# Four graph-attention layers on one core: the second half of each adjacency tile converted by POOL instead of DVE during the first pass

## What is computed

```python
h = jnp.einsum('nf,hfd->hnd', x, W)
e = jax.nn.leaky_relu(s_src[:, :, None] + s_dst[:, None, :], 0.01)
e = jnp.where(adj[None, :, :] == 0, -jnp.inf, e)
alpha = jax.nn.softmax(e, axis=-1)
out = jnp.einsum('hij,hjd->hid', alpha, h)
return jax.nn.elu(out)
```

## Time and profile before

| | |
|---|---|
| median of 3 runs | 3547.81 us (3545.58 to 3547.96) |
| the profiled execution's own time | 3546.96 us |
| its span | 3545.0 us |
| DVE busy over the span | 2442.6 us (69%) |
| PE busy over the span | 3075.2 us (87%) |
| POOL busy over the span | 1355.8 us (38%) |

### The profile page before, as it was taken

One profiled execution on the slowest core, in us unless ns is written; L12 is line 12 of the kernel. 1 busy time (PEld: TensorE's weight loads), 2 busy tenths in 40 slices (PEclk: granted clock), 3 DMA queues, 4 the chain that ended last, 5 costly groups with the idle time before them and its releaser, 6 DMA issues.

```text
span 3545.0 us, 75493 instructions
## 1 busy us (share of the span) xinstructions
PE 3075.2 (87%) x26666; PEld 2775.1 (78%) x26666; DVE 2442.6 (69%) x4181; ACT 1671.2 (47%) x2980; POOL 1355.8 (38%) x1770
## 2 busy tenths in 40 slices
PE   6688899999649999999969999968888888559998
PEld 5688899999639999999958888845565555449998
DVE  4888788887778888887765444347777777564446
ACT  4456788998548899889830000012222222230000
POOL 2433455532234555552210000025555555524443
PEclk9799999999879999999989999979999999779999
DMA  7564000000000000000010000010000000000001
GB/s 260 182 241 156 10 12 13 12 13 17 1 7 12 12 13 12 13 12 11 13 60 10 18 12 15 16 34 6 6 6 6 6 6 6 3 0 1 0 0 47
DMA packets 48448, 113.41 MB, mean 32 GB/s; under 512 B 8176, under 2 KB 29168, under 8 KB 40176
## 3 DMA queue, kind: packets, MB, share of 16 engines
q1 hardware_dynamic: 48368, 112.35, 9.5%
HBM read 103.75 MB, written 8.59 MB: 32 GB/s over the span
## 4 chain that ended last, share of the span: by engine, by line
PE 60%; DVE 23%; issue 8%; POOL 3%; DMA 2%; ACT 2%; DVEq 1%; SPq 1%; POOLq 0%; ACTq 0%
PE bank L933 15%; PE bank L936 15%; PE bank L988 11%; PE bank L939 10%; PE bank L998 6%; DVE sums L1408 4%; DVE rings L1463 3%; PE bank L897 2%; DMA arena<-in_adj_dram 2%; DVE rings L1466 2%; DVE srow L1569 2%; DVE sums L1563 1%; DVE vtmp_pool L1539 1%; POOL vtmp_pool L614 1%; PE bank L911 1%
## 5 line engine op out<-in xcount | busy, mean ns | idle before, releaser
L933 PE MATMUL bank<-values,rings 128*128 128x195 bf16 x8192 | 1420.2, 247 | 136.6 <-DVE rings L1466 77.7
L756 ACT ACTIVATE above<-srow,kpass 128x512 fp8e4<-128x512 f32 x2048 | 1292.9, 709 | 294.4 <-DVE rings L1466 278.7
L936 PE MATMUL bank<-values,rings 128*128 128x195 bf16 x8192 | 1420.6, 250 | 0.0
L933 PEld LDWEIGHTS bank<-values,rings 128*128 128x128 fp8e4 x8192 | 809.6, 99 | 155.6 <-issue 154.1
L936 PEld LDWEIGHTS bank<-values,rings 128*128 128x128 fp8e4 x8192 | 788.1, 96 | 1.1
L1463 DVE TENSOR_TENSOR rings<-rings,above 128x512 uint32<-128x512 uint32 x512 | 383.5, 749 | 237.9 <-PE bank L936 191.8
L988 PE MATMUL bank<-values 128*128 128x257 f32 x2048 | 445.4, 381 | 12.1 <-DVE values L1339 12.1
L988 PEld LDWEIGHTS bank<-values 128*128 128x128 f32 x2048 | 390.4, 191 | 66.9 <-issue 12.3
L1466 DVE TENSOR_TENSOR rings<-rings 128x512 uint32<-128x512 uint32 x512 | 409.5, 800 | 17.5
L939 PE MATMUL bank<-values,rings 128*128 128x195 bf16 x4096 | 348.1, 248 | 23.0 <-DVE rings L1454 23.0
L939 PEld LDWEIGHTS bank<-values,rings 128*128 128x128 fp8e4 x4096 | 347.7, 97 | 23.6 <-issue 23.4
(11 more groups left out here) (176 smaller groups left out, 3636.6 us busy)
## 6 DMA issues: line engine op xcount, KB each, us to landing
arena<-in_adj_dram SPq DMA_DIRECT2D x64, 1024.0 KB, 5.3
srow<-src_dram SPq DMA_DIRECT2D x72, 256.0 KB, 3.1
x<-in_x_dram SPq DMA_DIRECT2D x1, 4096.0 KB, 14.5
attn_dram<-rings SPq DMA_DIRECT2D x8, 512.0 KB, 2.9
values<-attn_dram SPq DMA_DIRECT2D x16, 256.0 KB, 2.6
out_dram<-x SPq DMA_DIRECT2D x8, 512.0 KB, 2.9
arena<-in_L_gnn_fe_w_dram SPq DMA_DIRECT2D x2, 512.0 KB, 9.0
arena<-in_L_gnn_W_hz_dram SPq DMA_DIRECT2D x1, 1024.0 KB, 9.2
```

What stands on the lines that cost most here:

```text
L756: last = act.activation(above[:, k % 2, q, :], srow[:, par, :], ACT.Relu, scale=BIG, bias=kpass[:, slot, q * BITS + k:q * BITS + k + 1], s ...
L933: pe.matmul(acc[:, 0:KW], pos[:, k % 2, q, :].bitcast(FP8)[:, rows], v[:, 0:KW], start=first, stop=final, skip_group_check=True)
L936: last = pe.matmul(acc[:, KW:2 * KW], neg[:, k % 2, q, :].bitcast(FP8)[:, rows], v[:, KW:2 * KW], start=False, stop=final, skip_group_chec ...
```

## The change

The semaphore that tells that a half is bf16 becomes two, one for each half, so SP and PE wait for each half on its own. DVE converts only half 0 in pass 0 (tiles 0 to 7 before it are still converted on DVE in both halves). POOL converts half 1 of the four tiles of a group: the first ahead of its value work of kind 0, the second behind kind 0, the third and fourth behind kind 1, ahead of the quotients.

```diff
-        s_adjbf = sem("adj_is_bf16")
+        s_adjbf = [sem("adj_is_bf16_0"), sem("adj_is_bf16_1")]
...
-                    sp.wait_ge(s_adjbf, t * 2 + (half - 1))
+                    sp.wait_ge(s_adjbf[half], t)
...
+            def convert(t):
+
+                pool.wait_ge(s_adj[1], (t + 1) * 16)
+                pool.wait_ge(s_packmm, t * 2 + 2)
+                pool.nop(nofuse=True)
+                pool.tensor_scalar(adj_bf[:, 1, :], adj_in[:, 1, :], 0, None, ALU.is_gt).then_inc(s_adjbf[1], 1)
...
+                    if l == 0 and p == 0:
+                        with pool.Fori(0, PACKING // 2) as gg:
+                            for par in range(2):
+                                g = gg * 2 + par
+                                t = gg * (2 * GT) + (PACKED_FIRST + par * GT)
+                                chain.enter(g, links)
+                                convert(t)
+                                for kind in range(kinds):
+                                    made = value_parts(pool, chain, vtmp_pool, kind, g * GT, GT, 1, 1)
+                                    if kind == 0:
+                                        convert(t + 1)
+                                made.then_inc(s_vals, 1)
+                                convert(t + 2)
+                                convert(t + 3)
+                                quotient(0, 0, g, par)
...
             def pack(t):
 
                 for half in range(2):
-                    pe.wait_ge(s_adjbf, t * 2 + half + 1)
+                    pe.wait_ge(s_adjbf[half], t + 1)
...
-            def convert(t):
-
-                for half in range(2):
+            def convert(t, halves=(0, 1)):
+
+                for half in halves:
                     dve.wait_ge(s_adj[half], (t + 1) * 16)
 
                     dve.wait_ge(s_packmm, t * 2 + (half + 1))
                     dve.tensor_scalar(adj_bf[:, half, :], adj_in[:, half, :], 0, None, ALU.is_gt)\
-                        .then_inc(s_adjbf, 1)
+                        .then_inc(s_adjbf[half], 1)
...
-                        convert(packing + k // 2)
+                        convert(packing + k // 2, (0,))
```

More of the change, by code:

```diff
@@ L580, in attention @@
                         pool.wait_ge(s_unit, p * UNITS + (CREDIT + TURN[l] * H * UNITS))
+                    if l == 0 and p == 0:
[13 more added lines that the diff above has]
+                                quotient(0, 0, g, par)
+                        with pool.Fori(PACKING // 2, NG // 2) as gg:
+                            for par in range(2):
+                                g = gg * 2 + par
+                                chain.enter(g, links)
+                                for kind in range(kinds):
+                                    made = value_parts(pool, chain, vtmp_pool, kind, g * GT, GT, 1, 1)
+                                made.then_inc(s_vals, 1)
+                                quotient(0, 0, g, par)
+                        chain.leave(NG)
+                        continue
                     with pool.Fori(0, NG // 2) as gg:
```

## The result

The changed kernel takes 3650.66 us (median of 4 runs, 3647.66 to 3652.43), the kernel before 3547.89 us in the same comparison. The ratio is 1.0287, with a 95% interval of 1.0274 to 1.0301: 103 us slower. The sign was forecast. The size was not: 3562 us was given, with a range that ended at 3635.

What follows compares the result with a forecast made beforehand. Packing groups were taken as paced by converting half 1, its load, and converting again. Five groups at +2.0 us (+10) and the clock's +4 added to 3546.96 gave 3561, or 3562 us against the runs' median; range 3545 to 3635 us.

Steps and rivals of the forecast that it cites:

- The operation's size: POOL's convert of half 1, 2048 elements: taken as 1.9 us, 2.5 us with waiting for DVE and semaphores.
- the upper row: Bound from above on POOL's convert, from L493's 0.527 us for 128 elements: 2.4 ns each, 5.1 us for 2048.
- the slow rival: POOL's tensor_scalar to bf16 is slow: 5.7 us a convert, groups 50.6 us, 3628 us in all; chance 0.25.
- POOL's place behind the quotients: A group's first POOL convert waits for the previous group's quotients, 5.2 us; PE stands 3.8 us longer.
- E: Time origin of a packing group in pass 0 of layer 0: the end of an evacuation.
- P0: End of PE's packing of a group's first tile: E + 5.1 us before, forecast at E + 8.9.
- the prediction's signs: What would show it: POOL's is_gt median 2.3 us, PE's first-pack wait 4 us, groups 37 to 39 us.
- The next three tiles: Tiles after a group's first: POOL's cycle of 5.5 us load plus 2.5 us convert, 8.0 us replacing 8.6.
- The two engines hold each other off: DVE and POOL share a port pair as exclusive lock; POOL's 1.9 us against DVE's saved 1.2, no gain counted.
- the rival of the sides: DVE's sides stand behind each POOL convert: +5 us a group, +25 in all, 3587 us; chance 0.12.
- Group 0: First packing group, no quotients ahead of its first convert: taken as 0, between -3 and +3 us.
- The clock: One more low-clock stretch of PE in each of five groups: +0.8 us each, +4 us in all.

Runs made afterwards that it cites:

- e_copy: The changed kernel with POOL's is_gt replaced by a tensor_copy of int32 to bf16 in the same place; 3567.96 us, ratio 1.0057.
- p_forms: The kernel before plus 22 POOL instructions alone behind all its work, eleven forms twice each; one-operation tensor_scalars took 5.4 us, copies 1.9 us.
- p_pairs: The kernel before plus lone POOL tensor_scalars behind its work, various operation pairs and singles; mult-add, mult-mult, add-mult 1.9 us, subtract-mult and max-add 7.1, singles 5.4.
- e_spare: The kernel before, DVE converting both halves, plus four POOL is_gt per group 0 to 5 whose results nobody reads; 3639.22 us, ratio 1.0258.
- e_hoist: The changed kernel, is_gt kept, first convert of each packing group moved ahead of the previous group's quotients; 3637.06 us, ratio 1.0255.
- e_act: ACT converts half 1 of tiles 8 to 31 by activation Copy, POOL as in the kernel before, two semaphores; 3546.3 us, ratio 0.9992.
- e_spare_copy: The kernel before plus four 1.9 us POOL copies per group 0 to 5, at the change's places, results unread; 3581.58 us, ratio 1.0091.

## Why the prediction was wrong

**The operation's size: wrong, and it is the step that failed.** I bounded POOL's convert by 1.9 and 5.1 us (8.4 with no fixed part) and took 1.9, because "three rows lie on that line" and L493 was the shortest. It measured 5.37 us alone and 5.68 in the mean: the price from the upper row, 5.1 us, was right to 5 per cent. With 1.9 us in that place (e_copy) the kernel takes 3568 us, with 5.4 us 3651. The three rows were a copy, a cast, and a tensor_scalar of two operations, L644. The added instruction is a tensor_scalar of one operation, and L493 was the one row of that kind with more than a few elements; L611, from which the working took the fixed part, belongs to it too. I looked at L493's output type, where the operations, their number and kind, were the difference (p_forms, p_pairs). The prediction's estimate of 1.76 us, from the Trainium skill ("GPSIMD Engine Reference", 3.1 Elementwise), does not hold for this instruction: the trace has 5.37 us for 2048 elements. It spoke against the slow rival, and wrongly.

**POOL's place behind the quotients: right.** In e_copy, where only the size is put right, half 1 of the first tile is copied out at 202.34, E + 9.1 with E = 193.26; P0 was forecast at E + 8.9. In the changed kernel it is copied out at 179.95, E + 13.4 with E = 166.55, where the slow rival had E + 12.1; DVE stands 7.1 us for it there and 8.7 at the longest, PE 5.7 and 7.3. In e_copy PE's own wait at that pack is 2.15 us, where the prediction's signs named 4: PE comes to it at E + 4.7 in place of E + 3.1, after a unit at a granted clock of 0.63.

**The next three tiles: the arithmetic right, the wait named wrong.** 8.0 us were forecast for a tile of the quick form; e_copy's groups bear it out as a sum. For the slow form POOL's cycle of load and convert is the slow rival's 11.2 us a tile (its converts begin at 183.30, 194.58 and 206.10), and there is a second cause, about as long, which I had as a rival of its own at 0.12 and with 1.9 us: the port.

**The two engines hold each other off: right in kind, and underpriced.** The earlier trace rows showed it, and I set POOL's 1.9 us against DVE's 1.2. I then counted neither. e_spare prices it: 0.7 us a group for each microsecond that POOL holds. The rule of the Trainium skill ("SBUF — State Buffer", Who interferes with whom) agrees with the timeline of group 1: a one-input tensor_scalar of DVE stood until POOL's instruction ended, and so did the one at 224.61 us of e_spare (it ended at 229.46, POOL's at 229.18). It agrees only in part for DVE's two-input tensor_tensor: the one at 236.04 was held up too, but it ended at 240.04, 1.2 us before POOL's instruction did (241.23). The prediction had set against the rival of the sides that POOL's converts fall 5 us behind a pack, "where PE has a unit in hand"; that can't cover 5.4 us, since a unit is 2.7.

**Group 0: wrong.** I took 0, and +6 us in the slow case; it was +16.2. The quotients are not ahead of POOL's convert there, but DVE is held off all the same: its own first convert, at 114.33, took 5.65 us in place of 1.2. PE waited 11.4 us for POOL's halves in this group, and its granted clock was 0.82 over it, 0.92 before. No run divides the 16.2 us among these.

**The clock: misjudged, in two places.** I gave it 0.8 us in each of five groups. e_copy's groups 2 and 3, at 0.95, came to 37.9 and 37.7 us without it. Where the level was lower it did show: group 6, which converts nothing, went from 27.4 us at 0.94 to 28.6 at 0.89, and PE's busy time rose by the same 1.2 us. That and groups 0 and 5 (38.1 and 41.4 us against 35.9 and 37.2) are most of what puts e_copy 6 us over my time. In the changed kernel it stands in the packs, here of the first and the last tile of group 1:

```profile
171.25 1.05 PE L943 MATMUL bank<-powers,arena 128*128 128x128 bf16 x16
177.96 1.87 PE L943 MATMUL bank<-powers,arena 128*128 128x128 bf16 x16 [5.65 <-POOL arena L542]
...
211.71 1.86 PE L943 MATMUL bank<-powers,arena 128*128 128x128 bf16 x16 [2.56 <-POOL arena L542]
```

Half a pack takes 1.05 us, and 1.87 us behind a wait of 5.65 us; the granted clock in that stretch is 0.50 (1.2 GHz).

**The slow rival,** at 0.25, said 5.7 us a convert, 50.6 us a group and 3628 us. Measured are 52 to 54 us and 3651. With group 0 at the price of the others, its own sum is 3547 + 6 x 14.8 = 3636. In group 1, which takes 52.5 us, the last 2 us lie at the ends: the first pack ended at E + 13.3 where 12.1 was in that sum, the three tiles behind it took 33.7 us (33.6 summed), and the rest 5.5 (4.9). POOL's half was ready at E + 11.2, just as summed, so the first pack came late in the main because it ran at the lower clock, 0.8 us. The waits and the port can't be told apart so: e_spare takes away the wait for the data and leaves 50.5 us, with four more converts on DVE; e_hoist takes away only the wait at the first tile, gives part of it back at the second, and leaves 49.3. The two prices hide in one another, and each of these mends gives back 2 to 4 us of 17.

## What to carry to other kernels

Before work goes to another engine, find the row with the same instruction, number of operations and kind included, and take that row even when it is small and stands alone; rows of the same engine with another instruction are not three votes. Where two engines share a port, moving work between them moves the hold too, so count both engines' port time as one sum (an upper bound here: 56 us were summed for e_spare's group, 50.5 measured), and read a 0.4 us instruction that shows 5.6 us of busy time as a wait. And a consumer's data must not stand in a queue behind something that waits for that consumer: hoisting it here shifted the wait to the next piece. Moving the waiting block itself, the quotients, is what no run here tried.

## What the runs showed of the hardware

- POOL's tensor_scalar on 128x2048: one operation 5.4 us (add, mult, max, is_gt), mult-add, mult-mult and add-mult 1.9, subtract-mult, max-add and is_gt-mult 7.1. Types did not matter. The cast from int32 to bf16 takes 1.9 us.
- ACT's Copy of 128x2048 int32 to bf16 takes 1.91 us. Beside the one at 206.40 us of e_act, DVE's sides took 0.42, 0.69 and 0.69 us, as undisturbed.
- DVE's casts and reduces from PSUM kept their 0.42 and 0.5 us beside POOL's long instructions (172.44 us of the changed kernel, 215.05 us of e_hoist). Its instructions that read SBUF and began soon behind a POOL tensor_scalar of 5.4 us did not: the 0.42 us tensor_scalars ended 0.3 us after it, the tensor_tensors 1.2 us before its end, and a tensor_tensor that began 4.2 us or more behind it took its usual 0.69 us. Behind a POOL copy of 1.9 us the tensor_tensors ended 0.5 us after it (e_copy, e_spare_copy).
